# An attention block on one core: where TensorE issues the products with the values among the scores

## What is computed

```python
h = layernorm(x)
q, k, v = h @ Wq, h @ Wk, h @ Wv
latent = (k + v) @ W_down_kv
k_rec, v_rec = latent @ W_up_k, latent @ W_up_v      # 16 heads of 8
scores = clip(q_h @ k_h.T * scale) * exp(-1e-4 * |i - j|)
attn = softmax(scores)                               # 1024 x 1024 a head
x = x + (attn @ v_h) @ Wo
x = x + fp8_product(layernorm(x), kernel) + bias
```

## Time and profile before

| what | us |
|---|---|
| median of 3 executions (526.9 to 529.14) | 526.92 |
| the profiled execution | 526.96 |
| its span, first to last instruction | 525.2 |
| ScalarE busy | 489.5 |
| TensorE matmuls busy | 487.2 |
| VectorE busy | 276.8 |

### The profile page before, as it was taken

One profiled execution on the slowest core, in us unless ns is written; L12 is line 12 of the kernel. 1 busy time (PEld: TensorE's weight loads), 2 busy tenths in 40 slices (PEclk: granted clock), 3 DMA queues, 4 the chain that ended last, 5 costly groups with the idle time before them and its releaser, 6 DMA issues.

```text
span 525.2 us, 9404 instructions
## 1 busy us (share of the span) xinstructions
PE 487.2 (93%) x3457; PEld 111.9 (21%) x3457; DVE 276.8 (53%) x641; ACT 489.5 (93%) x534; POOL 218.9 (42%) x285
## 2 busy tenths in 40 slices
PE   8799999999999999999999999999999999999961
PEld 3312111122122122122121211122121212121220
DVE  5524554556654654546645565454654564445646
ACT  3789999999999999999999999999999999999961
POOL 0889519791630249982450219993101121002110
PEclk9999999999999999999999999999999999999995
DMA  5589989947994103667976001747987000100000
GB/s 178 166 258 227 325 190 198 338 179 175 258 207 105 46 7 143 210 229 171 249 166 150 8 5 61 275 165 208 259 168 182 8 4 7 47 0 2 1 21 25
DMA packets 50467, 73.79 MB, mean 140 GB/s; under 512 B 6192, under 2 KB 29168, under 8 KB 50416
## 3 DMA queue, kind: packets, MB, share of 16 engines
q1 hardware_dynamic: 49600, 72.85, 50.5%
q10 hardware_dynamic: 816, 0.28, 0.2%
HBM read 35.40 MB, written 35.65 MB: 135 GB/s over the span
## 4 chain that ended last, share of the span: by engine, by line
PE 55%; ACT 31%; issue 7%; DVE 6%; DVEq 0%; ACTq 0%
ACT probs L760 30%; PE ps L960 27%; PE ps L944 16%; DVE ps L1183 3%; PE ps L828 2%; PE ps L824 2%; PE ps L940 2%; PE ps L833 1%; PE ps L861 1%; PE ps L856 1%; PE ps L799 1%; PE ps L868 0%; DVE xn L1231 0%; PE ps L818 0%; DVE stats L1099 0%
## 5 line engine op out<-in xcount | busy, mean ns | idle before, releaser
L760 ACT ACTIVATE probs<-ps 128x1024 f32<-128x1024 f32 x512 | 478.9, 1061 | 9.7 <-DVE ps L1183 6.1
L960 PE MATMUL ps<-probs,V 128*9 128x512 f32 x2048 | 267.8, 594 | 3.2 <-ACT probs L760 0.8
L1183 DVE TENSOR_TENSOR ps<-ps,consts 128x256 f32<-128x256 f32 (+1 forms) x256 | 144.3, 566 | 173.1 <-PE ps L944 166.0
L944 PE MATMUL ps<-Qs,Ks 64*128 64x512 bf16 x992 | 179.1, 385 | 13.8 <-ACT probs L760 7.2
L944 PEld LDWEIGHTS ps<-Qs,Ks 64*128 64x128 bf16 x992 | 42.7, 93 | 281.5 <-ACT probs L760 265.9
L960 PEld LDWEIGHTS ps<-probs,V 128*9 128x9 f32 x2048 | 31.3, 88 | 80.3 <-issue 60.4
L564 POOL TENSOR_SCALAR rs<-mv 128x4 f32<-128x4 f32 (+1 forms) x10 | 2.3, 229 | 102.7 <-DVEq L1365 102.2
L1191 DVE COPY pv_out<-ps 105x512 f32<-105x512 f32 x31 | 21.4, 692 | 33.9 <-PE ps L960 33.9
L647 POOL TENSOR_TENSOR xs<-xs,magic 128x512 f32<-128x512 f32 x7 | 8.9, 1277 | 70.4 <-DVE magic L1244 70.4
L598 POOL TENSOR_TENSOR sq<-sq,parts 128x1024 f32<-128x1024 f32 (+1 forms) x16 | 28.4, 1773 | 1.3
L600 POOL TENSOR_TENSOR parts<-sq,parts 128x1024 bf16<-128x1024 f32 (+1 forms) x16 | 28.3, 1771 | 1.3
(11 more groups left out here) (148 smaller groups left out, 281.4 us busy)
## 6 DMA issues: line engine op xcount, KB each, us to landing
Qs<-qp_dram SPq DMA_DIRECT2D x26, 512.0 KB, 9.5
qp_dram<-parts SPq DMA_DIRECT2D x14, 768.0 KB, 5.2
Ks<-kp_dram SPq DMA_DIRECT2D x26, 384.0 KB, 6.0
kp_dram<-parts SPq DMA_DIRECT2D x12, 384.0 KB, 3.6
kp_dram<-parts SPq DMA_DIRECT2D x6, 768.0 KB, 4.4
qp_dram<-parts SPq DMA_DIRECT2D x7, 512.0 KB, 6.6
X<-L_attn_x SPq DMA_DIRECT2D x10, 256.0 KB, 3.1
Qs<-qp_dram SPq DMA_DIRECT2D x10, 256.0 KB, 9.4
```

The lines of the kernel that those rows point to most:

```text
L760: nc.scalar.activation(probs[:, quad % RING, 2 * jp:2 * jp + 2, :].rearrange("p j n -> p (j n)"), ps_all[:, bank * CH:(bank + 2) * CH], AC ...
L944: last = nc.tensor.matmul(bank, Ks[half, g, jp, key_cols(v, kc)], Qs[half, g, jp, qh, v, :], start=True, stop=True)
L960: last = nc.tensor.matmul(pv[32 * j:32 * j + VW, :], V[:, unit // 2 * NB + kc, HG * j + g, :], probs[:, quad % RING, j, :], start=i == 0, ...
L1183: nc.vector.tensor_tensor(own, own, factors, ALU.mult).then_inc(fixed, 1)
```

## The change

```diff
                     elif quad > 0:
                         pe.wait_ge(exp_done, 2 * quad - 1)
+
+                    if quad >= 2 and s % 2 == 0 and not (in_f32 or variant(quad)[1] is not None):
+                        weigh(quad - 2)
                     qk(s)
-                    if quad >= 2 and s % 2 == in_f32:
+                    if quad >= 2 and s % 2 == 1 and (in_f32 or variant(quad)[1] is not None):
                         weigh(quad - 2)
```

## The result

The changed kernel takes 576.11 us (median; 575.51 to 577.37) against 527.65 beside it: a ratio of 1.092, with a 95% interval from 1.089 to 1.094. Slower by 48.5 us; the forecast was 578 and the range 561 to 591. The profiled execution took 575.65 us.

The account below looks back on a forecast made before the run. Bound: TensorE's order, whether each slot's scores are there when ScalarE comes. 120 pairs at 3.74 (448.8) plus jobs 54.9 make 503.7 instead of 452.5 us; 51.2 on 526.96 gives 578, range 561 to 591.

Parts of the forecast that it names:

- The chain from slot 1 to slot 2: TensorE and ScalarE, exponential's end through scores and both quads' products to slot 2's exponential: 3.74 us against ScalarE's 3.67, no cover.
- products to products: TensorE, start of one quad's products to the next quad's: taken as 0.86 us, bounded from above by 0.98.
- Jobs cost their own time and 0.12 more: 60 TensorE jobs between two quads' products from quad 16 on: uncovered, 47.7 us plus 60 x 0.12, together 54.9.
- Transposes of rows: Five TensorE jobs between two quads' products: 0.66 us long, 0.59 each to the next instruction.
- spreads of sums: TensorE jobs between two quads' products, counted with query and key projections: 19 at 1.05 us each.
- sums of squares: Four TensorE jobs between two quads' products: 1.00 us each, plus 0.12 for products to job.
- The sum: Slots 31 to 511: 120 pairs of quads at 3.74, 448.8, plus 54.9 for jobs: 503.7 us against 452.5, 51.2 more.
- small jobs: Five TensorE jobs without a row, put between the two kinds of transposes at 0.4 us each.
- The bounds: Whole kernel: 7 us more, 11 and 8 less, up to 6 more from VectorE; 559 to 591, taken as 561 to 591.
- What would show it: Profile: 50 to 60 us idle ahead of exponentials, released by line 944, not VectorE; 0.1 without a job, 0.5 to 1.3 with.
- fewer changes of kind would pay: Rival, TensorE: 0.12 + 0.11 saved per pair of quads, 28 us of its time; kernel faster at 514 us; chance 0.02.
- The granted clock: Rival: longer TensorE idling, some 0.8 us, drops its clock to 1.2 GHz, beyond 900 us; chance 0.02.

Follow-up runs that it names:

- the other way round: Kernel before with products ahead of both slots in quads to be fixed, behind both in the others: 636.97 us, 1.200 of the kernel before.

## Why the prediction was right, point by point

- **The chain from slot 1 to slot 2.** Put at 3.74 us without a job, 3.73 measured. The one term that no row of before showed, products to products, was taken as 0.86 from two passes; the changed kernel has 1.90 for sixteen matmuls against 1.04 for eight, 0.86.
- **Jobs cost their own time and 0.12 more.** Transposes of rows: 4.43 - 3.73 = 0.70 against 0.12 + 0.59; spreads of sums 4.90 - 3.73 = 1.17 against 0.12 + 1.05. The sums of squares were put too high: 0.85 (below) against 1.12. They stand between products without a loss, which I had put on every job; over four jobs that is 1.1 us.
- **The sum.** From slot 31 to 511 the prediction had 503.7 us. Line 760 over these slots in the changed kernel (durations in ns, first and last start):

```profile
L760 ACT ACTIVATE probs<-ps x481: 1017/1026/1045, 51.1 to 551.9; 128x1024 f32<-128x1024 f32 x161
```

  551.9 - 51.1 = 500.8, against 452.5 in the earlier trace rows: 48.3 more, which is nearly the whole result (48.7 by the profiled executions); head, first quads and tail hardly changed. The 2.9 us by which the sum was high are 1.5 of rounding (some 0.012 in each of 120 pairs), 1.1 in the sums of squares, and the rest in the small jobs, whose 0.4 each no row of before showed: the three transposes cost 0.63 a pair and the two of the check 0.43 and 0.03, against 0.52.
- **The bounds.** The lower one was for a saving that did not come: a job followed by products costs as much as one followed by scores (309.33 to 310.39, 1.06), and products to a job 0.97 (308.36 to 309.33). Only the sums of squares have it.
- **What would show it.** ScalarE's idle of 50 to 60 us, 56.6; releaser line 944, 51.6 of it. Behind a job the idle is 0.39 to 1.16 against 0.5 to 1.3. VectorE's part was to all but vanish: 6.1 us became 2.8, and all of that lies ahead of slot 31. One reading was wrong: I expected 0.1 us of idle in the pairs without a job too. The waits have 61 entries, 59 of them from slot 31 on, one for each of the 60 jobs but the smallest (line 852):

```profile
ACT probs L760 <- PE ps L944: 51.6, 61, 1.2
...
ACT probs L760 <- DVE ps L1186: 2.8, 4, 1.1
```

  ScalarE's starts run ahead of its ends, so a delay so small leaves no idle; it is seen in the round of 3.73 only, 0.06 over ScalarE's own 3.67.
- **The rivals.** That fewer changes of kind would pay is false as a forecast of the time, though its price is real: by the starts of its rows the change takes about 0.2 us a pair off TensorE, a little less than the 0.12 + 0.11 of the prediction, and its busy time fell from 487.2 to 469.6 us; TensorE spends that time waiting. The granted clock stayed at 1.00 from 45 to 548 us with idle times of 0.59 and 0.75, as the first quads with their 0.95 suggested; in the other way round, where two idle times of about 1 us come close together, it did fall, so the 0.95 of the first quads was no assurance for every order.

## What to carry to other kernels

When two engines feed each other through a few buffers, don't count an engine's work or its changes of kind: write down, for each buffer, the chain from its release to the end of the work that it is needed for, and compare that with the time that the consumer gives (here three slots, 2.75 us, and four for a whole round). Whatever is put into a chain without cover costs its full time, as the jobs did here, and two moves that cost 1.5% each can cost 9% together. The same few sums then tell where to put the work instead.

## What the runs showed of the hardware

In these rows TensorE's loss at a change of kind goes by the shape of the array's tiles, not by the data type. In the changed kernel the f32 sums of squares (32 columns a tile, like the products' 9 in groups of 32) stand between the products with no loss at all, while f32 jobs over 128 columns have it on both sides (from a spread of sums to the products it is 1.06, where two spreads in a row take 1.91, so 0.86 for one with its like behind it), and bf16 jobs over 128 columns have it ahead of them as well (line 868):

```profile
144.27 0.39 PE L944 MATMUL ps<-Qs,Ks 64*128 64x512 bf16 x2 [0.59 <-ACT probs L760]
144.59 1.04 PE L960 MATMUL ps<-probs,V 128*9 128x512 f32 x8
145.45 1.04 PE L842 MATMUL ps<-sq,consts 128*32 128x512 f32 x8
146.31 1.04 PE L960 MATMUL ps<-probs,V 128*9 128x512 f32 x8
147.28 0.82 PE L944 MATMUL ps<-Qs,Ks 64*128 64x512 bf16 x6
148.85 0.39 PE L944 MATMUL ps<-Qs,Ks 64*128 64x512 bf16 x2 [0.75 <-ACT probs L760]
...
156.62 1.05 PE L960 MATMUL ps<-probs,V 128*9 128x512 f32 x8
157.60 0.40 PE L868 MATMUL ps<-eye,xn 128*128 128x128 bf16 x4
```

Products to sums of squares take 0.86 and these to products 0.86, as products to products; products to the scores take 0.97, products to the bf16 job 0.98. The round is 148.85 - 144.27 = 4.58 long, 0.85 over one without a job. The Trainium skill (TensorEngine Tiling (Array Packing), Key Properties) says that a change of tiling mode drains the engine; the trace agrees, and puts some 0.11 us on a change behind products.

The second finding is the clock of the other way round: behind two idle times of about 1 us with 1.36 of work between them it fell to its lower level at 9 of 30 seams and stayed at 1.00 at the others. It also stayed at 1.00 with single ones of 0.95 in the first quads and of up to 0.75 in each round of the changed kernel.
